# Four graph convolutions: 17 gathered blocks and a dense matrix of 32 in place of 15 and 34

## What is computed

```
# layer 1 (one convolution), norm = d[src] * w * d[dst]
out = segment_sum(norm[:, None] * (h @ W)[src], dst) + b
# layer 3 (three convolutions in a row)
h  = x @ W_init
x1 = relu(conv(h,  W1) + h)
x2 = relu(conv(x1, W2) + h)
x3 = conv(x2, W3) + h
# conv(x, W) = segment_sum(norm[:, None] * (x @ W)[src], dst) + b
```

## Time and profile before

| | us |
|---|---|
| median of 3 runs | 6823.73 |
| lowest and highest | 6820.10, 6828.18 |
| the profiled execution, its own time | 6820.84 |
| its span, first to last instruction | 6819.0 |
| mean granted clock | 0.843 |

### The profile page before, as it was taken

One profiled execution on the slowest core, in us unless ns is written; L12 is line 12 of the kernel. 1 busy time (PEld: TensorE's weight loads), 2 busy tenths in 40 slices (PEclk: granted clock), 3 DMA queues, 4 the chain that ended last, 5 costly groups with the idle time before them and its releaser, 6 DMA issues. The chain is left out here.

```text
span 6819.0 us, 113163 instructions
## 1 busy us (share of the span) xinstructions
PE 5493.8 (81%) x30494; PEld 4417.2 (65%) x30494; DVE 3783.5 (55%) x13003; ACT 2171.3 (32%) x7007; POOL 4607.1 (68%) x4391
## 2 busy tenths in 40 slices
PE   2988998538769999885886996666666699999998
PEld 2777787536667777774775995665666455555555
DVE  6555562288975555223887445666666644344343
ACT  4333334268943333333995003222222300000000
POOL 1777677678857777777886661777777267276473
PEclk9777678678967777876997998888888799999999
DMA  6888875656734444335444884555555489899997
GB/s 217 256 276 277 261 214 160 116 104 138 142 68 102 105 103 105 80 80 54 77 76 117 287 288 139 165 157 157 158 158 157 79 289 307 287 305 299 302 304 256
DMA packets 903995, 1231.39 MB, mean 181 GB/s; under 512 B 230601, under 2 KB 640861, under 8 KB 890407
## 3 DMA queue, kind: packets, MB, share of 16 engines
q1 hardware_dynamic: 607544, 887.00, 41.0%
q0 software_dynamic: 207392, 219.55, 17.9%
q10 hardware_dynamic: 88428, 117.57, 5.1%
HBM read 987.45 MB, written 237.38 MB: 180 GB/s over the span
## 5 line engine op out<-in xcount | busy, mean ns | idle before, releaser
L1033 POOL DMA_INDIRECT ACC<-table,TABS x1760 | 1696.9, 964 | 628.2 <-issue 603.0
L1348 POOL DMA_INDIRECT BUF<-table,TABS x840 | 799.3, 952 | 581.6 <-issue 245.6
L1114 POOL DMA_INDIRECT adjacency<-TABS x600 | 966.9, 1612 | 311.5 <-issue 260.2
L1033 POOL DMA_INDIRECT BUF<-table,TABS x880 | 841.5, 956 | 331.5 <-issue 331.5
L1805 PE MATMUL picked<-ident,ACC 128*128 128x128 f32 (+1 forms) x3520 | 890.7, 345 | 0.0
L1804 PE MATMUL picked<-G,OH 128*128 128x128 f32 (+1 forms) x2352 | 619.6, 356 | 203.9 <-DMA ACC<-table,TABS 110.8
L2185 PE MATMUL asum<-BUF 128*128 128x144 f32 x3520 | 561.2, 305 | 165.6 <-DVE BUF L2163 162.6
L1805 PEld LDWEIGHTS picked<-ident,ACC 128*128 128x128 f32 (+1 forms) x3520 | 673.2, 222 | 0.0
L1804 PEld LDWEIGHTS picked<-G,OH 128*128 128x128 f32 (+1 forms) x2352 | 431.6, 218 | 342.1 <-issue 315.8
L1708 PE MATMUL sums<-BUF,G 128*128 128x128 f32 x1760 | 320.0, 339 | 399.0 <-DVE ACC L1063 398.7
L2185 PEld LDWEIGHTS asum<-BUF 128*128 128x128 f32 x3520 | 476.4, 197 | 196.4 <-issue 182.1
(11 more groups left out here) (397 smaller groups left out, 10318.8 us busy)
## 6 DMA issues: line engine op xcount, KB each, us to landing
TABS<-adjacency SPq DMA_DIRECT2D x272, 512.0 KB
BUF<-in_edge_pair SPq DMA_DIRECT2D x880, 128.0 KB
BUF<-adjacency SPq DMA_DIRECT2D x102, 1024.0 KB
BUF<-adjacency SPq DMA_DIRECT2D x204, 512.0 KB
adjacency<-zeros ACTq DMA_DIRECT2D x44, 1792.0 KB
G<-adjacency SPq DMA_DIRECT2D x136, 512.0 KB
kept<-ACC SPq DMA_DIRECT2D x220, 272.0 KB
G<-kept SPq DMA_DIRECT2D x220, 272.0 KB
```

What stands on the lines that cost most here:

```text
L1033: po.indirect_dma_start(rows[:, slot, j, 0:width], None, tab, bass.IndirectOffsetOnAxis(ap=SRC[:, q * GT + j:q * GT + j + 1], axis=0)).the ...
L1114: po.indirect_dma_start(adj_flat, bass.IndirectOffsetOnAxis(ap=PLACE[:, k:k + 1], axis=0), TOTAL[:, k:k + 1], None, compute_op=ALU.add).th ...
L1348: po.indirect_dma_start(R[:, q % deep_ring, j, :], None, table, bass.IndirectOffsetOnAxis(ap=SRC[:, k:k + 1], axis=0)).then_inc(S(f"gather ...
```

## The change

`LIGHT` goes from 15 to 17, and with it by the formulas of lines 51 to 57: `HEAVY` from 34 to 32, `DENSE` from 9 chunks to 8 that are all four wide, `NEAR` from 70 groups to 78, `FAR` from 150 groups to 142. The blocks stay in 13 parts, now five gathered (the fifth with one block) and eight dense. A pass of layer 3 has 200 units in place of 213, layer 1's pass 104 in place of 111. The places of the near groups are set anew, and the transfers that add are shared out anew.

```diff
-LIGHT = 15
+LIGHT = 17
 HEAVY = NB - LIGHT
 NEAR_TILES = LIGHT * (E + CYCLE * (P - 1)) // (CYCLE * P)
 NEAR = -(-NEAR_TILES // (2 * GT)) * 2
 FAR = GROUPS - NEAR
-FIRST_FAR = 80
+FIRST_FAR = 76
...
-MERGES = ((4, 11, 56, 9), (4, 4, 52, 10))
+MERGES = ((4, 11, 53, 8), (4, 4, 49, 9))
...
-            places = near_by(6, 1.3)
+            places = near_by(6, 1.2)
             assert places[-1] < len(units)
...
-            places = near_by(12, 2.5)
+            places = near_by(12, 2.08)
             assert places[-1] < ends[DENSE - 2]
```

## The result

| | before | with the change |
|---|---|---|
| median | 6825.95 us (4 runs) | 6916.64 us (4 runs) |
| lowest and highest | 6820.10, 6840.52 | 6892.84, 6925.14 |
| span of the profiled execution | 6819.0 | 6891.0 |
| mean granted clock | 0.843 | 0.852 |

The changed kernel takes 1.0126 times as long, with a 95% interval from 1.0109 to 1.0143. The forecast was 6903 us in a range from 6870 to 6935.

What follows compares the result with a forecast made beforehand. PE was taken as only just slower than POOL, with POOL bounding layer 3's passes after the change. 6820.84 + 96 - 15 - 1 = 6900.8 us for the profiled execution, so 6903 us for the median, range 6870 to 6935.

Steps and rivals of the forecast that it cites:

- POOL's pace: Layer 3's three passes: POOL, at 5.03 us a near group against PE's 4.39, delays the last near groups, +95 us.
- the lag: Layer 3's passes: from last gather's start to last near group on PE, 5.5 us, before 19.4, 11.9 and 10.7.
- The step: Layer 3's passes: time from one gather to the next on POOL, 1.256 us, staying as before.
- PE's lead: Layer 3's passes: a start of about 10 us, used up after some 16 of the 78 near groups.
- The tails and boundaries: Layer 3, behind each pass's last near group: -3 us for three tails, +4 us for last parts and boundaries.
- the +4 for the doubled short steps of the last part: Layer 3's pass ends: last part of four blocks, not two, and two more stores, +4 us, bounds 0 and +9.
- Layer 1's pass: Layer 1: narrow chunk's products removed, 8 near groups added, PE still later than POOL; -15 us, bounds -17 and -4.
- The adding transfers: Layer 0's weighted sums and the stages behind them: 32 fewer transfers, POOL waits anyway; -1 us, bounds -8 and 0.
- PE did not go on bounding: Rival, layer 3's passes: PE stays the bound if POOL issues a near group in 4.39 us; 6766 us, chance 5%.
- The merges: Rival, layer 0's adding transfers: they were on the path, up to 60 us come back, about 6845 us; chance 5%.
- The clock: Rival, layer 3's passes: PE's clock falls to 0.80 as it stops before nearly every near group; 7053 us, chance 5%.
- The signs: Changed kernel's profile: 312 gathers in 391 us a pass, PE near 90%, gather waits of 35 to 55 us a pass.

Runs made afterwards that it cites:

- finish_early: Changed kernel with layer 1's dense parts finished and squared behind their own chunks, except the first, not behind the last near group; 6903.0 us.
- all_early: Changed kernel with near groups every 2.3 units and early finishing of dense parts in layers 3 and 1; 6793.8 us, on a slow chip 8281.8.

## Why the prediction was right, and where it wasn't

**POOL's pace, right.** The last near groups were to come 26.3, 33.8 and 35.0 us later and came 25.0, 33.0 and 34.0 later; the lag was to be 5.5 and is 4.7 to 5.2 us. The step is 1.255, not 1.256. PE's lead was to last 16 groups; in the first pass the first wait for a gather is at the 21st. In the second and third there was no lead to use up: the first group already stands 5.1 and 4.2 us behind its last gather, and waits come at the first group and from the 5th on. Since the last near group is set by POOL's pace from the first gather on, the forecast did not need the lead, but the waits are unequal by it: 22.7 us in the first pass, 32.0 and 33.2 in the others. Three runs show that this is the cause and no coincidence: fewer gathers give the time back, cheaper ones give back their own share, and the order alone costs it without any added gather.

**The tails and boundaries, too dear by 11 us.** The terms were -3 and +4, measured is -10.3 for both. PE's part from the last near group to the next pass's first unit shrank by 3.4 and 1.8 us (63.2 and 63.5), and from there to the first gather it did not grow: 16.5 and 18.2 us, before 19.6 and 18.2. The term that failed is the +4 for the doubled short steps of the last part (bounds 0 and +9): no lengthening shows, the first boundary is 3.1 us shorter, the second unchanged. What made the first one shorter was not looked into.

**Layer 1's pass, -3.9 for -15.** Just outside its bounds of -17 to -4, and for a reason that the working had wrong: "the finishing of the last chunk is a microsecond longer" looked at the last chunk alone. The finishing of all 49 blocks starts behind the last near group, and the narrow chunk had covered ACT's squares. PE's share was -13.2 for -16.

**The adding transfers, right in kind.** The stage between the halves lost 2.2 us (from its first adding transfer to the next gather 74.9, now 72.7, and 72.7 again in the six other profiles with 17 blocks from the first chips); POOL's last transfer now ends at 1987.3, 7 us ahead of DVE's last work. The last stage of layer 0 lost 1.0 in this profile and nothing steady over the others. The rest of the -6.6 is in the two logits stages, which differ as much between runs of one kernel: the first ends between 1283.8 and 1308.3 us in those seven profiles with 17 blocks.

**The rivals.** PE did not go on bounding (the step stayed). The merges gave 2 to 3 us and not 60. The clock held 0.99, 1.00 and 0.99 in the three passes, in spite of 113 waits of up to 2.5 us: what the Trainium skill tells of short idle spells (TensorE: Matmul & The Clock Gate, A second HAM failure mode: psum-queue depth-cycling) did not come about here.

**The signs.** Promised were 312 gathers in 391 us (390.2), pass to pass 467 and 481 us (462.6 and 475.6, the tails again), PE at 90% (94, 92 and 90), and waits of some 0.6 us before most near groups, 35 to 55 us a pass. The records show 113 waits of PE for gathers in 234 groups, 88.0 us, 29 a pass: fewer than half of the groups and less than promised. The weight loads ahead of them waited 179 times, 219.8 us, 73 a pass, so the promise lies between the two counts. The prediction also calls POOL's steps "without a pause"; its own rows have a gap of 0.30 us behind each 0.95, so the track is busy three quarters of the time even while POOL is the bound.

**The sum.** The terms give +80 us on the profiled execution, and it came to +72.0. That it came so near is in part luck: the tails were 11 us too dear and layer 1's pass 11 us too cheap, and the two cancel. The rest is 3 us less in the gathering stretches and 6 us less ahead of layer 1's pass. (The bounds as listed add up to 6889 and 6932, a little wider above than the 6888 to 6928 that the prediction made of them.) The median lies 23.8 us above that execution's own time, since this was the shortest of its four runs; in the kernel before 5.1 lie between them. By the medians the change costs 90.7 us, and the forecast of 6903 is 14 us short. I read this as scatter between runs, which the first logits stage alone has to that amount. The other three runs show a mean clock of 0.842 to 0.844, this one 0.852, and finish_early, whose layer 3 is the same program, spent 1426.8 us in it against 1427.1 here while its first logits stage took 22 us longer. But the other three runs have no profile, so it is argued and not shown.

## What to carry to other kernels

An engine that is busy 60% of a stage may still be at its full pace: divide the stretch from its first to its last instruction by their number, and if the step is constant and its gaps wait for nothing, shifting work to it costs that step, whatever its busy share. When two engines are within 2% of each other, places in the instruction order should follow the slower one's pace (here 130 us hung on it), and what PE would otherwise wait for should stand ahead of the wait, not behind it. When work that another engine's finishing hid behind is taken away, count that finishing whole, from the moment at which it may start.

## What the runs showed of the hardware

An indirect gather on POOL took 0.900 us for 64 rows of 512 bytes and 0.947 for 128, each with a gap of 0.30 us behind it: halving the rows saved 5% of the instruction. The same program runs in 6791 us on one chip and in 8284 on another, with the gathers at the same 0.947 us; the mean granted clock is 0.844 on the one and 0.775 on the other, PE waits 30 us for nothing that the profile shows in the first pass there and not at all on the first chip, and a gain of 0.56% turns into a loss of 0.58%. Behind one large store (24 blocks, in all_early) the next transfer on ACT's queue took 4.57 us to issue in the second pass (4.49 in the first), where the median is 0.34.
